# Top-64 attention in groups of four heads: where ScalarE drains the scores of the last two heads, and a settling path written as a loop

## The reference

```python
dots = jnp.einsum('bhid,bhjd->bhij', q, k) * SCALE          # 16 heads, 16 memory keys + the tokens
dots = jnp.einsum('bhij,hk->bkij', dots, pre_proj)
dots = jnp.where(causal, NEG_INF, dots)
topk_vals = jax.lax.top_k(dots, 64)[0]
thresh = topk_vals[..., -1:]
dots = jnp.where(dots < thresh, NEG_INF, dots)              # keep the 64 largest of each row
attn = jax.nn.softmax(dots, axis=-1)
out = jnp.einsum('bhij,bhjd->bhid', attn, v)
```

## Time and profile before

| | us |
|---|---|
| median of 3 runs | 3037.24 |
| lowest, highest | 3037.17, 3040.78 |
| the profiled execution | 3029.58 |
| its span, first to last instruction | 3027.1 |
| VectorE busy | 2415.8 (80%) |
| TensorE busy | 2302.1 (76%) |
| ScalarE busy | 1414.6 (47%) |
| from the first stage's start to the last mask (330 to 2726 us of the span) | 2396 |

### The profile page before, as it was taken

One profiled execution on the slowest core, in us unless ns is written; L12 is line 12 of the kernel. 1 busy time (PEld: TensorE's weight loads), 2 busy tenths in 40 slices (PEclk: granted clock), 3 DMA queues, 4 the chain that ended last, 5 costly groups with the idle time before them and its releaser, 6 DMA issues.

```text
span 3027.1 us, 34365 instructions
## 1 busy us (share of the span) xinstructions
PE 2302.1 (76%) x10182; PEld 1328.8 (44%) x10182; DVE 2415.8 (80%) x9392; ACT 1414.6 (47%) x2143; POOL 5.2 (0%) x43
## 2 busy tenths in 40 slices
PE   6696545657767757778888888988984888884897
PEld 3554323333434424444444444544542545442564
DVE  2506688889888988989899999999998988884445
ACT  1121223444445435555565666666663666652221
POOL 0000000000000000000000000000000000000000
PEclk7798667777878878899998999999997999987898
DMA  2000000000000000000000000000000000001000
GB/s 59 1 0 1 1 1 1 1 1 1 2 1 1 1 1 1 1 1 1 1 1 1 1 1 1 1 1 1 1 1 1 1 1 1 1 1 49 1 1 14
DMA packets 15509, 12.20 MB, mean 4 GB/s; under 512 B 6892, under 2 KB 13686, under 8 KB 15222
## 3 DMA queue, kind: packets, MB, share of 16 engines
q1 hardware_dynamic: 11184, 6.82, 0.9%
q10 hardware_dynamic: 4038, 2.37, 0.3%
HBM read 8.14 MB, written 1.05 MB: 3 GB/s over the span
## 4 chain that ended last, share of the span: by engine, by line
DVE 53%; PE 30%; ACT 8%; issue 7%; DVEq 2%; ACTq 0%
DVE cand L1106 13%; DVE R L1155 7%; DVE r L1157 7%; PE bank L823 6%; PE bank L791 6%; PE bank L903 4%; DVE W L1136 4%; DVE F L1176 4%; DVE W L1135 4%; ACT R L543 4%; PE bank L807 3%; ACT R L536 3%; PE bank L911 2%; DVE WP L1170 2%; PE bank L808 1%
## 5 line engine op out<-in xcount | busy, mean ns | idle before, releaser
L823 PE MATMUL bank<-WP,Y 128*128 128x512 f32 x1088 | 685.4, 718 | 152.0 <-ACT WP L550 151.2
L807 PE MATMUL bank<-ident,R 128*128 128x128 f32 x2176 | 524.0, 315 | 248.8 <-ACT R L543 246.6
L1106 DVE MAX8 cand<-R 128x8 f32<-128x12 f32 (+15 forms) x4096 | 642.6, 226 | 5.3 <-ACT R L521 4.2
L791 PE MATMUL bank<-hT,qT 128*128 128x512 f32 (+3 forms) x1280 | 533.1, 555 | 37.3 <-ACT R L521 22.2
L807 PEld LDWEIGHTS bank<-ident,R 128*128 128x128 f32 x2176 | 346.2, 159 | 465.6 <-issue 214.7
L550 ACT ACTIVATE WP<-bank 128x512 f32<-128x512 f32 x544 | 320.8, 594 | 369.8 <-PE bank L808 368.6
L808 PE MATMUL bank<-nidentb,F 128*128 128x128 bf16 x2176 | 466.3, 240 | 0.0
L536 ACT ACTIVATE R<-R,cutb 128x144 f32<-128x144 f32 (+15 forms) x256 | 310.2, 1212 | 294.1 <-DVEq L1148 292.5
L521 ACT ACTIVATE R<-bank 128x1024 f32<-128x1024 f32 (+7 forms) x384 | 290.5, 774 | 278.6 <-PE bank L791 168.3
L1155 DVE SCALAR_TENSOR_TENSOR R<-R,r 128x144 f32<-128x144 f32 (+15 forms) x256 | 350.3, 1368 | 9.2 <-DVE r L1154 0.2
L543 ACT ACTIVATE R<-R,negm 128x144 f32<-128x144 f32 (+15 forms) x256 | 289.8, 1205 | 123.9 <-DVEq L1254 123.7
(11 more groups left out here) (225 smaller groups left out, 2164.1 us busy)
## 6 DMA issues: line engine op xcount, KB each, us to landing
R<-in_L_attn_Wkv ACTq DMA_DIRECT2D x2, 512.0 KB, 8.0
R<-in_L_ffn_gate_w SPq DMA_DIRECT2D x1, 1024.0 KB, 7.7
R<-in_L_ffn_up_w SPq DMA_DIRECT2D x1, 1024.0 KB, 10.3
out<-X SPq DMA_DIRECT2D x1, 1024.0 KB, 5.1
R<-in_L_attn_Wq ACTq DMA_DIRECT2D x1, 512.0 KB, 6.1
WP<-in_L_attn_Wo ACTq DMA_DIRECT2D x1, 512.0 KB, 10.5
R<-in_L_ffn_wi SPq DMA_DIRECT2D x1, 256.0 KB
R<-in_L_ffn_wo SPq DMA_DIRECT2D x1, 256.0 KB
```

Source lines behind the costliest of these rows:

```text
L791: last = pe.matmul(to, qT[:, k % 2, i, :], hT[:, a:b], start=True, stop=b < n, skip_group_check=True)
L807: pe.transpose(to[:, P * i:P * i + P], S[:, k % NS, i, blk], ident[:, :])
L823: pe.matmul(bank[6], Y[:, j, :], PT[:, (blocks_before(k) + j) % 4, :], start=(j == 0), stop=(j == k // 4))\
L1106: mark(dve.max(cand[:, :, c, i], lists(S[:, k % NS, i, 0:n], n, c)))
```

## The change

Of each group's scores, ScalarE drains `m` and units 0 and 1 where it did (`drain_early`), but unit 2, the queries and unit 3 one stage later: one slot behind each of the four exponentials of that stage, and what is left behind the fourth (`drain_late`). `late_from` gives the number of slots that stay early. TensorE's and VectorE's orders of work stay as they are, so all of their waits on `s_sdrain` stay too.

`settle` is now one function for the group: it finds the four units' flags at once (two transposes), then loops over the four units with a register loop (`Fori`), loads each flag, and in the doubtful unit copies the row, runs 7 rounds of MAX8 and MATCH_REPLACE8 in an inner register loop, and one more MAX8. It is jumped over on the same condition as before. The flag tile grows from 1 to 5 columns.

```diff
--- before.py
+++ after.py
@@ -201,7 +201,7 @@
         full = sb("full", [P, 2])
         doubt = sb("doubt", [32, 4 * GU])
         doubts = sb("doubts", [32, 2, 32])
-        flag = sb("flag", [1, 1], mybir.dt.int32)
+        flag = sb("flag", [1, 1 + GU], mybir.dt.int32)
         rden = sb("rden", [P, GU])
         bob = sb("bob", [P, P])
         ident = sb("ident", [P, P])
@@ -521,9 +521,21 @@
                     act.activation(S[:, k % NS, i, MEM + SC * c:MEM + SC * c + w], src[:, 0:w], ACT.Copy)\
                         .then_inc(s_sdrain, 1)
 
-            def drain_scores(k):
-                for name in plan_slots():
-                    if name[1] == k and name[0] != "q" or name[0] == "q" and name[1] == k + 1:
+            def slots_of(k):
+                return [name for name in plan_slots()
+                        if name[1] == k and name[0] != "q" or name[0] == "q" and name[1] == k + 1]
+
+            def late_from(k):
+
+                return 1 + 2 * slots(k // 4)
+
+            def drain_early(k):
+                for name in slots_of(k)[:late_from(k)]:
+                    drain_slot(name)
+
+            def drain_late(k, first, last=None):
+                if k < NG:
+                    for name in slots_of(k)[late_from(k):][first:last]:
                         drain_slot(name)
 
             def count_above(k, i):
@@ -559,15 +571,20 @@
                 act.activation(Zs[:, :], bank[6], ACT.Copy).then_inc(s_zs, 1)
 
             drain_slot(("q", 0, 0, 0))
-            drain_scores(0)
-            drain_scores(1)
+            drain_early(0)
+            drain_late(0, 0)
+            drain_early(1)
             for p in range(NG + 1):
                 turns = list(range((p - 1) // 4 + 1)) if p >= 1 else []
                 if p >= 1:
                     for i in range(GU):
                         exponent(p - 1, i)
+                        drain_late(p + 1, i, i + 1)
+                    drain_late(p + 1, GU)
                     for j in turns[0:3]:
                         drain_turn(p - 1, j)
+                else:
+                    drain_late(1, 0)
                 if p < NG:
                     for i in range(GU):
                         count_above(p, i)
@@ -578,7 +595,7 @@
                         drain_turn(p - 1, j)
                     drain_rest(p - 1)
                 if p + 2 < NG:
-                    drain_scores(p + 2)
+                    drain_early(p + 2)
 
 
             def fdrain(name, dst, func=ACT.Copy, **kw):
@@ -1175,27 +1192,38 @@
                 n = wide(k // 4)
                 mark(dve.tensor_scalar(F[:, i, 0:n], S[:, k % NS, i, 0:n], thr[:, i:i + 1], 4.0, ALU.is_lt, ALU.mult))
 
-            def settle(k, i):
+            def settle(k):
+
 
                 n = wide(k // 4)
-                dve.tensor_reduce(doubts[:, 0, 0:1], doubt[:, i::GU], AX.X, ALU.max)
+                rest, eight = A[:, 1, 0:n], r9[:, 0, 1:9]
+                dve.drain()
+                dve.tensor_reduce(doubts[:, 0, 0:GU], doubt[:, :].rearrange("p (g i) -> p i g", i=GU), AX.X, ALU.max)
                 dve.drain()
                 dve.transpose(doubts[:, 1, :], doubts[:, 0, :])
                 dve.drain()
-                dve.tensor_reduce(flag[:, :], doubts[0:1, 1, :], AX.X, ALU.max)
+                dve.tensor_reduce(doubts[:, 0, 0:1], doubts[:, 1, :], AX.X, ALU.max)
                 dve.drain()
-                row, rest, m_ = S[:, k % NS, i, 0:n], A[:, 1, 0:n], r9[:, i, 1:9]
-                with dve.If(dve.value_load(flag[0:1, 0:1], min_val=0, max_val=1) != 0):
-                    for r in range(8):
-                        dve.max(m_, rest if r else row)
+                dve.transpose(doubts[:, 1, :], doubts[:, 0, :])
+                dve.drain()
+                dve.tensor_copy(flag[:, 1:1 + GU], doubts[0:1, 1, 0:GU])
+                dve.drain()
+                with dve.Fori(0, GU) as i:
+                    row = R[:, bass.ds(i * WIDE + (k % NS) * GU * WIDE, n)]
+                    with dve.If(dve.value_load(flag[0:1, bass.ds(i + 1, 1)], min_val=0, max_val=1) != 0):
+                        dve.tensor_copy(rest, row)
                         dve.drain()
-                        if r < 7:
-                            dve.match_replace(rest, m_, rest if r else row, 2 * FILL)
+                        with dve.Fori(0, TOPK // 8 - 1):
+                            dve.max(eight, rest)
                             dve.drain()
-                    dve.tensor_copy(thr[:, i:i + 1], m_[:, 7:8])
-                    dve.drain()
-                    dve.tensor_scalar(F[:, i, 0:n], row, thr[:, i:i + 1], 4.0, ALU.is_lt, ALU.mult)
-                    dve.drain()
+                            dve.match_replace(rest, eight, rest, 2 * FILL)
+                            dve.drain()
+                        dve.max(eight, rest)
+                        dve.drain()
+                        dve.tensor_copy(thr[:, bass.ds(i, 1)], eight[:, 7:8])
+                        dve.tensor_scalar(F[:, :, :].rearrange("p i n -> p (i n)")[:, bass.ds(i * WIDE, n)], row, eight[:, 7:8],
+                                          4.0, ALU.is_lt, ALU.mult)
+                        dve.drain()
 
             def threshold(k):
                 t = k // 4
@@ -1241,15 +1269,13 @@
                 judged = done[0]
                 mask(k, 2)
                 dve.wait_ge(s_dve, judged)
-                mark(dve.tensor_reduce(flag[:, :], doubts[0:1, 1, :], AX.X, ALU.max))
+                mark(dve.tensor_reduce(flag[:, 0:1], doubts[0:1, 1, :], AX.X, ALU.max))
                 judged = done[0]
                 mask(k, 3)
                 dve.wait_ge(s_dve, judged)
                 doubtful = dve.value_load(flag[0:1, 0:1], min_val=0, max_val=1)
                 with dve.If(doubtful != 0):
-                    dve.drain()
-                    for i in range(GU):
-                        settle(k, i)
+                    settle(k)
                 dve.wait_ge(s_dve, done[0])
                 dve.sem_inc(s_lose, 1)
```

## The result

The changed kernel takes 2920.14 us (median of 4 runs, 2912.89 to 2921.19) against 3037.2 us before: a ratio of 0.961, 95% interval 0.959 to 0.963. That is 117 us saved where 74 were forecast, and 15 us under the low end of the range.

The account below looks back on a forecast made before the run. VectorE sets the pace to about 2140 us, then the ScalarE-TensorE loop is level and in the last seven or so stages ahead. 72 - 5 + 14 - 5 - 2 = 74 us off 3037.2 gives 2963 us, range 2935 to 2998.

Parts of the forecast that it names:

- The cause of the gaps: Ahead of `top`: a jump over 204 instructions leaves the two held blocks of about 120, so code is fetched, some 2.3 us.
- Rival B: At the jump over `settle`: the stall stays, from any taken jump or the flag loads; 3027 us, chance 0.10.
- Part 1: Jump over the settling path, 330 to 2140 us: a shorter jump makes all gaps short, 72 us saved, less 5.
- The 5 us for fetches still under way: At the shorter jump: a block entered within 2.3 us ahead costs 1 us in a tenth of the stages.
- My upper bound, 72: Most that the shorter jump over the settling path could save, in us; the lower bound was 0.
- Part 2: ScalarE's order of drains: 1.6 us saved in each of stages 53 to 61, 14 us, between -13 and 40.
- one of 4.3: TensorE in stage 61: one idle piece of 4.3 us, x + 4.1 to x + 8.4, before the fourth exponential.
- Part 3: VectorE's lists wait for the moved drains: half a microsecond in each of ten stages up to 54, -5 us.
- Part 4: The settling loop when it runs, in two doubtful groups: -2 us for both, at most -53 us.
- Rival C: Settling loop's backward jumps fetch code: the two doubtful groups pay up to 53 us; 2985 to 3015 us, chance 0.08.
- Rival D: TensorE's clock falls in every stage of t >= 12, VectorE's lists wait 6 us each; 3047 us, chance 0.06.
- the loop's best case: ScalarE's order of drains at its best end, 40 us in place of 14: 2937 us.

Follow-up runs that it names:

- the three paddings: Changed kernel with 85, 150 or 215 more instructions in the settling path, jumped over in 62 of 64 groups: 2938.23, 3012.84 and 3090.46 us.
- the loop alone: Changed kernel's settling path as a loop, with ScalarE's drains in the order of the kernel before: 2956.65 us, ratio 0.973 to the kernel before.
- the clock alone: Kernel with the looped settling path and old drain order, plus useless TensorE matmuls ahead of the exponentials in groups 48 to 63: 2932.15 us, ratio 0.967.
- the order alone: Kernel before with ScalarE's new order of drains, the settling path still written out four times: 3016.34 us, ratio 0.992.

## Why the prediction was wrong

**The cause of the gaps was right,** and so was what the change does to them: the three paddings and the packet in every long gap show it, and 122 packets came where some 130 were foretold. The Trainium skill's warning (Runtime: NRT & Kernel Launch, Instruction fetch mechanics), that a jump out of the two held pages stalls, agrees with every run; its page size of 256 instructions does not: with that size neither a jump of 208 nor one of 191 would have stalled, and 38 and 27 did. Rival B is out.

**Part 1 was mis-sized: 72 - 5 forecast, 81 measured.** The step was "all short they would be 52 x 0.76 = 39.5". I priced the new gaps by the old short ones. But every old short gap is the landing of a jump of 208 in the next block, with its 0.3 us; my sentence that such a landing costs nothing more was wrong. A jump of 41 mostly stays in its block: in 29 of the 39 jumps up to stage 40 the record behind the branch comes 0.16 or 0.17 us after it, in ten 0.45 to 0.53. The 52 gaps sum to 29.9 us (mean 0.58), and 111.3 - 29.9 is 81.4 us. The 5 us for fetches still under way did not occur. My upper bound, 72, was thus no bound.

**Part 2 failed in its working: 14 us forecast, 36.5 measured.** The step that failed is "unit 3's matmuls wait for the drained queries". The wait is for the queries of the unit's own group, and those were drained a stage earlier; the queries drained among the late slots are those of the group after. Stage 60 of the changed kernel, ScalarE, then TensorE:

```profile
2433.14 1.02 ACT L521 ACTIVATE R<-bank 128x1024 f32<-128x1024 f32 x1 [0.75 <-PE bank L810]
2434.06 1.90 ACT L555 ACTIVATE R<-R,negm 128x1936 f32<-128x1936 f32 x1
2435.86 1.01 ACT L521 ACTIVATE R<-bank 128x1024 f32<-128x1024 f32 x1
2436.76 1.91 ACT L555 ACTIVATE R<-R,negm 128x1936 f32<-128x1936 f32 x1
2438.56 1.02 ACT L521 ACTIVATE R<-bank 128x1024 f32<-128x1024 f32 x1
2439.47 1.91 ACT L555 ACTIVATE R<-R,negm 128x1936 f32<-128x1936 f32 x1
2441.27 0.60 ACT L510 ACTIVATE qT<-bank 128x512 f32<-128x512 f32 x1
2441.74 1.92 ACT L555 ACTIVATE R<-R,negm 128x1936 f32<-128x1936 f32 x1
2443.54 1.95 ACT L521 ACTIVATE R<-bank 128x1024 f32<-128x1024 f32 x2
2446.82 1.28 ACT L562 ACTIVATE WP<-bank 128x512 f32<-128x512 f32 x2 [1.33 <-PE bank L825]
```

```profile
2436.93 1.16 PE L790 MATMUL bank<-hT,G 128*128 128x128 f32 x8 [0.28 <-ACT R L521]
2439.73 1.96 PE L808 MATMUL bank<-hT,qT 128*128 128x512 f32 x4 [1.64 <-ACT R L521]
2441.92 1.98 PE L808 MATMUL bank<-hT,qT 128*128 128x512 f32 x4 [0.24 <-ACT qT L510]
...
2443.89 1.12 PE L858 MATMUL bank<-MV,PmT 64*128 64x512 f32 x2
2444.94 1.16 PE L861 MATMUL bank<-M,Zs 128*128 128x128 f32 x8
2445.94 0.27 PE L824 MATMUL bank<-ident,R 128*128 128x128 f32 x1
...
2447.47 1.12 PE L840 MATMUL bank<-WP,Y 128*128 128x512 f32 x2
```

x is 2434.16, the end of unit 1's last drain (line 1). TensorE fills unit 3's first slot at 2439.73, as soon as unit 2's second drain, 2438.56 to 2439.58, frees the slot, and the second at 2441.92 behind the drained queries. Its pauses are 0.28, 1.64 and 0.24 us and not one of 4.3, and the exponentials no longer hold it: the first turned block is drained at 2446.82, x + 12.7, where the old order has x + 16.3. At full width, in stage 61, it is x + 13.0, where the forecast had x + 15.2 and the old order x + 16.8. Two products take 1.12 us, not 2.02, the clock having stayed at 2.4 GHz in stages 60 and 61. In stages 57 to 59 it fell to 1.2 GHz for 3.4 us each, where the old order had 6.8 to 10.2 us in every stage from 57 on.

The second fault of part 2 is the number of stages. I let the order count in nine stages from 53 on. With the gaps gone from VectorE, the loop of ScalarE and TensorE overtakes it in stage 49: the loop alone has 274.2 us in stages 49 to 54 as before, the changed kernel 261.7. In all, from 49 to 62, the order takes 12.5 + 3.4 + 22.5 = 38 us off the loop alone. How it divides into place and clock can't be given as a sum, since they overlap: the clock alone, with the drains in their old place, gives 24.5 us; the place with most of the clock gives 36.5. What the place gives at the same clock was not run.

**Part 3 was right in kind and too large:** VectorE's lists wait 3.8 us for ScalarE, in six waits in stages 58 to 62, where the mask had waited before; 10 to 40 us of waiting were foretold. In the stages up to 54, which I had charged with 5 us, they don't wait at all. What the 3.8 us cost can't be told from these runs; the loop alone has 1.4 us of such waits in stages 59 to 62. With all drains behind the exponentials the same wait was 53.5 us.

**Part 4 was -2 and is -3.5 us** (stage 26 59.3 us instead of 57.2, stage 55 87.8 instead of 86.4; against the order alone, with 85.1 us in stage 55, it is 4.8 us). The path with the loop in group 26:

```profile
1045.56 0.63 DVE L1214 COPY R<-R 128x912 f32 x1 [1.11 <-issue]
1046.34 1.11 DVE L1217 MAX8 r<-R 128x8 f32<-128x912 f32 x1
...
1047.60 1.09 DVE L1219 MATCH_REPLACE8 R<-r,R 128x912 f32<-128x912 f32 x1
1049.08 1.11 DVE L1217 MAX8 r<-R 128x8 f32<-128x912 f32 x1 [0.38 <-issue]
...
1066.54 0.69 DVE L1224 TENSOR_SCALAR F<-R,r  x1
1071.13 0.27 DVE L1136 TENSOR_REDUCE top<-cand 128x4 f32<-128x64 f32 x1 [3.90 <-issue]
```

A backward jump of the inner loop costs 0.34 to 0.38 us ahead of its MAX8, not 2.4; the copy of the row 0.63 us. Behind the doubtful unit, the tests of the three others and the way out stand in one gap of 3.90 us. The sequencer's records divide it: three passes of the outer loop of 1.18 us each, and the way out; no backward jump has a stall of 2.4 us. Rival C is out.

**Rival D** asked for a clock that falls in each late stage. It rose. What D described, late drains that make TensorE and VectorE wait, is what the kernel with all of them behind the exponentials does, and even that kernel is faster than the one before.

The range missed since its low end took the loop's best case, 40 us, which the order nearly reached, but no value of part 1 above 72.

## What to carry to other kernels

Code that is almost never executed still has a price where it is longer than what the engine holds ahead: count its instructions, and if a jump over it has gaps of two sizes, a loop or a shorter body takes the long ones away. When one engine's stalls are removed, work out anew from which stage on the next loop leads; here two parts that gave 81 and 21 us alone gave 117 together. Put an engine's drains of another engine's results between its own long instructions, so that the other engine's pauses stay short; and check in the code which group a semaphore's count belongs to before a wait goes into a sum.

## What the runs showed of the hardware that was not expected

VectorE's jump over up to about 126 instructions never stalled, one over 256 always did, with 2.2 to 2.8 us more idle time each, and its instructions came in packets of 128. A landing in the next block cost 0.3 us more than one in the same: 1.08 us in stage 5 of the changed kernel against 0.77 to 0.79 in stages 2 to 4, and 1.10 to 1.12 in these three with 85 instructions more.

With the loop alone, TensorE's clock fell to 1.2 GHz in stage 60 during the second of four pauses (0.86, 1.35, 1.22 and 1.22 us, with one transpose and one mask matmul between them) and came back 6.8 us later. In the changed kernel it fell for 3.4 us in stages 57 to 59, about when a pause of 1.54 to 1.64 us ended, and stayed at 2.4 GHz in stages 60 and 61 with pauses like them (0.28, 1.64 and 0.24 us; 0.39, 1.75 and 0.34 us). Why the one and not the other, these traces do not show. With useless matmuls in the pauses the clock stayed at 2.4 GHz from stage 57 to 62, and 24.5 us were gained, 22.9 of them in the stages from 49 on.
